# Neighbour maximum in a graph kernel: word numbers added on TensorE, keys by five wide VectorE operations

## What is computed

```
mask = adj != 0
nm[i, f] = max over j with mask[i, j] of x[j, f]      # 0 if the row has no neighbour
x = layernorm(x + nm)
```

## Time and profile before

| | |
|---|---|
| median of 3 runs | 4908.32 us (4907.93 to 4910.63) |
| span of the profiled execution | 5439.8 us |
| PE busy in that span | 4559.6 us (84%) |
| DVE busy | 4311.2 us (79%) |
| ACT busy | 2207.6 us (41%) |
| POOL busy | 1205.9 us (22%) |
| mean granted TensorE clock | 0.929 |

### The profile page before, as it was taken

How to read it: one execution, slowest core, us unless ns; L and a number is a source line. 1 busy time by engine, 2 the same in 40 slices (tenths; PEclk the granted TensorE clock), 3 DMA queues, 4 the chain that set the end, 5 groups by cost and what they waited for, 6 DMA issues and landing times. The chain is left out here.

```text
span 5439.8 us, 68010 instructions
## 1 busy us (share of the span) xinstructions
PE 4559.6 (84%) x22263; PEld 2172.7 (40%) x22263; DVE 4311.2 (79%) x7371; ACT 2207.6 (41%) x2430; POOL 1205.9 (22%) x1342
## 2 busy tenths in 40 slices
PE   4766776677667766579999999999999999999999
PEld 3333333333333333323443333454444445444444
DVE  6666676667666667788888888889999987999998
ACT  3444444444444444398888888410000001000000
POOL 5555445454444455200000000000000000000000
PEclk6888888888888889889999999999999999999999
DMA  7555555555555555233232332122222202212220
GB/s 272 195 187 184 192 197 185 187 182 194 186 179 188 193 169 166 95 130 122 105 126 111 113 127 105 64 102 83 75 84 79 81 9 99 102 70 98 76 96 14
DMA packets 181695, 709.72 MB, mean 130 GB/s; under 512 B 31168, under 2 KB 39872, under 8 KB 132224
## 3 DMA queue, kind: packets, MB, share of 16 engines
q1 hardware_dynamic: 110816, 566.01, 29.3%
q0 software_dynamic: 33760, 73.21, 4.2%
q10 hardware_dynamic: 36864, 67.13, 3.5%
HBM read 630.59 MB, written 79.82 MB: 131 GB/s over the span
## 5 line engine op out<-in xcount | busy, mean ns | idle before, releaser
L1750 PE MATMUL bank<-w,GX 128*128 128x512 f32 x4096 | 1768.4, 593 | 4.8 <-DVE w L1865 4.8
L1865 DVE SCALAR_TENSOR_TENSOR w<-q,E,m 128x512 f32<-128x512 f32 x2048 | 1472.1, 758 | 130.8 <-PE bank L1750 39.1
L356 POOL DMA_INDIRECT ring<-x_ext,idx x1051 | 1032.8, 983 | 1074.2 <-DVE X L619 316.8
L1750 PEld LDWEIGHTS bank<-w,GX 128*128 128x128 f32 x4096 | 777.7, 191 | 975.3 <-issue 975.2
L607 DVE TENSOR_TENSOR top<-top,sums 128x1024 f32<-128x1024 f32 x484 | 589.2, 1217 | 626.7 <-remote 364.8
L507 PE MATMUL sums<-lone,xs 128*128 128x512 fp8e4 x3000 | 838.3, 421 | 287.0 <-DVE top L607 214.9
L1200 PE MATMUL acc<-w,GX 128*128 128x512 f32 x2048 | 939.6, 605 | 65.8 <-DVE w L1458 62.6
L430 ACT ACTIVATE stage<-tp 128x1024 fp8e4<-128x1024 uint16 x512 | 523.7, 1025 | 1088.1 <-remote 598.3
L1458 DVE SCALAR_TENSOR_TENSOR w<-q,E,u 128x1024 f32<-128x1024 f32 x512 | 634.7, 1274 | 1.9 <-PE acc L1200 1.8
L507 PEld LDWEIGHTS sums<-lone,xs 128*128 128x128 bf16 x3000 | 291.5, 105 | 814.7 <-issue 607.4
L1200 PEld LDWEIGHTS acc<-w,GX 128*128 128x128 f32 x2048 | 371.9, 190 | 564.5 <-issue 413.5
(11 more groups left out here) (250 smaller groups left out, 2919.3 us busy)
## 6 DMA issues: line engine op xcount, KB each, us to landing
adjb<-in_adj SPq DMA_DIRECT2D x256, 1024.0 KB
m<-mask_t SPq DMA_DIRECT2D x128, 1024.0 KB, 4.8
mask_t<-stage ACTq DMA_DIRECT2D x256, 256.0 KB
den_m<-mask_t SPq DMA_DIRECT2D x64, 1024.0 KB, 6.9
keep_m<-mask_t SPq DMA_DIRECT2D x64, 1024.0 KB, 4.9
ring<-x_ext,idx POOLq DMA_INDIRECT x1051
z<-row_scores SPq DMA_DIRECT2D x30, 256.0 KB, 4.6
xt_rows<-XT SPq DMA_DIRECT2D x8, 512.0 KB, 4.7
```

What stands on the lines that cost most here:

```text
L356: pool.indirect_dma_start(ring[:, s, :], None, x_ext, bass.IndirectOffsetOnAxis(ap=idx[:, k, s:s + 1], axis=0)).then_inc(done, 16)
L1750: last = nc.tensor.matmul(acc[b][:, :], GX[:, j, :], w[:, j % WR, :], start=(j == 0), stop=(j == T - 1))
L1865: nc.vector.scalar_tensor_tensor(out=w[:, j % WR, :], in0=q, scalar=E[:, j:j + 1], in1=m[:, b, j, :], op0=ALU.max, op1=ALU.mult).then_inc( ...
```

## The change

PE now adds a word's number to its code inside `tally`. Ahead of block 0 and ahead of block 4 of each tile's counts, one matmul with a stationary `one_row` and 512 moving columns of `numbers` starts the bank; the 16-column counts then accumulate onto it. The number is 0 to 255 within each half of the 512 words, times 2^-7. The `opens` activation of ACT is gone. On DVE the wide operations up to the list are now: exponent of the code (TENSOR_SCALAR, in place of L686), code minus it (L706's place), the number OR-ed into 448 of the 512 keys, the minimum of those 448 with `before` (whose nonzero entries are now 2^20), and a MAX8 for each half of 256. L711, L712, L716, L717 and the single MAX8 of L719 go. The release `cnt_used` moves from L706's place to the minimum, since that one still reads `tally`. The sums L701 and L772 go: `due` and `found` come from `accum_out` of the operations before them. The small operations work on 16 values instead of 8 (two on the numbers, the same five in the loop over depth), and their keys (64 with a row of blanks) go into the 64 free places of the 512 keys, so that the sorting rounds run over 512 instead of 536.

```
+LEAST = 2.0
+HALVES = 2
+HW = NW // HALVES
+NUMBER = 2.0 ** -7
+BEFORE = 2.0 ** 20
+MORE = 8 * HALVES
...
@@ POOL, once @@
+            word_steps = Steps(pool, words_numbered)
+            word_steps.did(nc.gpsimd.iota(half_no[:, :, :], pattern=[[HW, HALVES], [0, 8]], base=0, channel_multiplier=0))
+            word_steps.do(nc.gpsimd.memset(one_row_f, 0.0))
+            word_steps.do(nc.gpsimd.affine_select(out=one_row_f, in_=one_row_f, compare_op=ALU.not_equal, fill=1.0, base=0, pattern=[[0, P]], channel_multiplier=1))
...
@@ ACT, phase @@
-                if 1 <= t <= T:
-                    act.wait_ge(counted, t)
-                    nc.scalar.activation(opens[:, :, 1:WPG], before, ACT.Relu, bias=top_bit[:, 0:1], scale=-TOP_BIT).then_inc(opens_made, 1)
...
@@ PE @@
+            pe.wait_ge(numbers_made, 1)
...
             def count(q, k, e):
+                if e % (T // TRB // HALVES) == 0:
+                    bank = slice(e * TRB, e * TRB + T // HALVES)
+                    nc.tensor.matmul(tally[:, bank, :].rearrange("p t c -> p (t c)"), one_row[:, :], numbers[:, :, :].rearrange("p t c -> p (t c)"),
+                                     start=True, stop=False, skip_group_check=True)
                 for g in range(e * TRB, (e + 1) * TRB):
-                    last = nc.tensor.matmul(tally[:, g, :], stage[:, q, g, k * P:(k + 1) * P], powers[:, :], start=True, stop=True)
+                    last = nc.tensor.matmul(tally[:, g, :], stage[:, q, g, k * P:(k + 1) * P], powers[:, :], start=False, stop=True, skip_group_check=True)
...
@@ DVE, once @@
+            steps.did(nc.vector.memset(many_high[:, :, :], 0.0))
+            steps.do(nc.vector.memset(numbers[:, :, :], 0.0))
+            dve.wait_ge(words_numbered, 3)
+            steps.do(nc.vector.tensor_scalar(numbers[:, :, 0:WPG], code_no[:, 0:HW].rearrange("p (t w) -> p t w", w=WPG), NUMBER, None, ALU.mult))
+            nc.vector.tensor_copy(one_row[:, :], one_row_f).then_inc(numbers_made, 1)
...
@@ DVE, phase @@
+                not_opening = keys[:, :, 1:WPG]
+                listed = keys[:, :, :].rearrange("p g w -> p (g w)")
...
                 if extracts:
                     hold(dve, counted, s + 1)
-                    hold(dve, opens_made, s + 1)
-                    steps.did(nc.vector.tensor_tensor(out=bits(by_group(high)), in0=bits(code_ps), in1=bits(opens[:, :, :]), op=ALU.bitwise_and))
-                    side.did(nc.vector.tensor_scalar(junk, cnt, -1.0, 0.0, ALU.add, ALU.max))
+                    steps.did(nc.vector.tensor_scalar(bits(keys[:, :, :]), bits(code_ps), EXPONENT, None, ALU.bitwise_and))
+                    side.did(nc.vector.tensor_scalar(junk, cnt, 1.0, -float(T), ALU.max, ALU.add, accum_out=due[:, bass.ds(s, 1)]))
                     side.did(nc.vector.tensor_reduce(deg[:, bass.ds(s, 1)], cnt, axis=AXX, op=ALU.add))
...
-                if extracts:
-                    side.settle()
-                    side.did(nc.vector.tensor_reduce(due[:, bass.ds(s, 1)], junk, axis=AXX, op=ALU.add))
                 step(1)
                 if extracts:
                     steps.settle()
                     side.settle()
-                    nc.vector.tensor_tensor(out=by_group(x), in0=code_ps, in1=by_group(high), op=ALU.subtract).then_inc(cnt_used, 1)
+                    steps.did(nc.vector.tensor_tensor(out=by_group(x), in0=code_ps, in1=keys[:, :, :], op=ALU.subtract))
+                    steps.settle()
+                    side.did(nc.vector.tensor_tensor(out=bits(not_opening), in0=bits(not_opening), in1=by_group(code_no[:, :])[:, :, 1:WPG], op=ALU.bitwise_or))
                 if finishes:
                     into(old, 0, 2).then_inc(lower_free, 1)
                 if extracts:
-                    hold(dve, cnt_used, s + 2)
-                    steps.do(nc.vector.tensor_scalar(bits(high), bits(x), EXPONENT, None, ALU.bitwise_and))
-                    steps.did(nc.vector.tensor_tensor(out=x, in0=x, in1=high, op=ALU.subtract))
+                    steps.settle()
+                    side.settle()
+                    nc.vector.tensor_tensor(out=not_opening, in0=not_opening, in1=before, op=ALU.min).then_inc(cnt_used, 1)
                 step(2)
                 if extracts:
-                    steps.settle()
-                    steps.did(nc.vector.tensor_tensor(out=bits(x), in0=bits(x), in1=code_no[:, :], op=ALU.bitwise_or))
-                    side.did(nc.vector.tensor_tensor(out=bits(high), in0=bits(high), in1=code_no[:, :], op=ALU.bitwise_or))
-                    steps.settle()
-                    steps.did(nc.vector.max(out=y, in_=x))
+                    for a in range(HALVES):
+                        steps.did(nc.vector.max(out=y[:, 8 * a:8 * a + 8], in_=x[:, a * HW:(a + 1) * HW]))
...
-                    later = keys[:, NW:NW + (DEEP - 1) * MORE].rearrange("p (d n) -> p d n", n=MORE)
+                    later = keys[:, :, 0].rearrange("p (d n) -> p d n", n=MORE)
...
-                    side.did(nc.vector.scalar_tensor_tensor(out=pad[:, :], in0=srt[:, :], scalar=1.0, in1=row_no[:, 0:1].to_broadcast([P, SRT]), op0=ALU.is_lt, op1=ALU.mult))
+                    side.did(nc.vector.scalar_tensor_tensor(out=pad[:, :], in0=srt[:, :], scalar=LEAST, in1=row_no[:, 0:1].to_broadcast([P, SRT]), op0=ALU.is_lt, op1=ALU.mult, accum_out=found[:, bass.ds(s, 1)]))
...
-                    side.did(nc.vector.tensor_reduce(found[:, bass.ds(s, 1)], pad[:, 0:SLOTS], axis=AXX, op=ALU.add))
```

More of the change, by code:

```diff
@@ L206, in neighbour_max @@
         codes = sb("codes", [P, NW], F32)
-        opens = sb("opens", [P, T, WPG], F32)
-        top_bit = sb("top_bit", [P, 1], F32)
-        keys = sb("keys", [P, NW + (DEEP - 1) * MORE], F32)
+        numbers = sb("numbers", [P, T // HALVES, COLS], BF16)
+        one_row = sb("one_row", [P, P], BF16)
+        half_no = sb("half_no", [P, HALVES, 8], I32)
+        keys = sb("keys", [P, T, WPG], F32)
         many = sb("many", [P, MORE], F32)
+        many_i = sb("many_i", [P, MORE], I32)
         many_no = sb("many_no", [P, MORE], I32)
-        many_high = sb("many_high", [P, DEEP - 1, MORE], F32)
+        many_high = sb("many_high", [P, T // MORE, MORE], F32)
         srt = sb("srt", [P, SRT], F32)
@@ L234, in neighbour_max @@
         need_ps = tp[1][0:1, 0, 0:8].bitcast(F32)
-        high = keys[:, 0:NW]
+        one_row_f = merged[:, 2 * P:3 * P]
         low_half = adjb[:, :, :].bitcast(BF16).rearrange("p h (n two) -> p h n two", two=2)[:, :, :, 0]
@@ L252, in neighbour_max @@
         counted = sem("counted")
-        opens_made = sem("opens_made")
-        opens_free = sem("opens_free")
+        words_numbered = sem("words_numbered")
+        numbers_made = sem("numbers_made")
         cnt_used = sem("cnt_used")
@@ L292, in neighbour_max @@
         lowest = codes[:, 0:T]
-        bn = keys[:, 0:6 * T].rearrange("p (t s) -> p t s", s=6)
+        bn = keys[:, :, :].rearrange("p g w -> p (g w)")[:, 0:6 * T].rearrange("p (t s) -> p t s", s=6)
         @block.sync
@@ L657, in row_statistics, with phase @@
                 rows_done.settle()
-            def phase(t, k, extracts=True, finishes=True, quad=None, tops=True):
+            def phase(t, k, extracts=True, finishes=True, quad=None, turned=True):
                 s = t - 1
@@ L663, in phase @@
                 h = HALF
-                tops = tops and quad is not None and k == 0
+                turned = turned and quad is not None and k == 0
                 def bits(ap):
@@ L722, in phase @@
                     steps.settle()
-                    steps.did(nc.vector.tensor_scalar(many_no[:, :], bits(y), NW - 1, None, ALU.bitwise_and))
+                    steps.did(nc.vector.tensor_scalar(many_i[:, :], y, 1.0 / NUMBER, None, ALU.mult))
                 if finishes:
@@ L728, in phase @@
                     steps.settle()
-                    steps.did(nc.vector.tensor_tensor(out=bits(y), in0=bits(y), in1=many_no[:, :], op=ALU.bitwise_xor))
+                    steps.did(nc.vector.scalar_tensor_tensor(out=many_no[:, :], in0=many_i[:, :], scalar=HW - 1, in1=half_no[:, :, :].rearrange("p a n -> p (a n)"),
+                                                             op0=ALU.bitwise_and, op1=ALU.bitwise_or))
                 if finishes:
@@ L750, in phase @@
                 if extracts:
-                    later = keys[:, NW:NW + (DEEP - 1) * MORE].rearrange("p (d n) -> p d n", n=MORE)
-                    steps.did(nc.vector.tensor_tensor(out=bits(later), in0=bits(many_high[:, :, :]), in1=many_no[:, :].unsqueeze(1).to_broadcast([P, DEEP - 1, MORE]), op=ALU.bitwise_or))
+                    later = keys[:, :, 0].rearrange("p (d n) -> p d n", n=MORE)
+                    steps.did(nc.vector.tensor_tensor(out=bits(later), in0=bits(many_high[:, :, :]), in1=many_no[:, :].unsqueeze(1).to_broadcast([P, T // MORE, MORE]), op=ALU.bitwise_or))
+                    hold(dve, cnt_used, s + 2)
                     side.settle()
                     steps.settle()
```

(10 more changed lines are left out.)

14 lines of the change are left out of this document (4 added, 10 removed).

## The result

The changed kernel takes 4935.4 us (median of 4 runs, 4933.1 to 4937.0), the kernel before beside it 4908.1 us: ratio 1.0059, 95% interval 1.0045 to 1.0073. The change makes the kernel slower by about 27 us, and 4937 was forecast.

A forecast was written before the change was run, and what follows sets the result against it. Layer 0 was taken as bound by PE and DVE handing one buffer to and fro. Terms 0.39 + 0.04 + 0.05 = 0.48 us a tile, x 60 = 29 us on 4908.3, gave 4937 us; range 4892 to 4972.

The forecast's parts named there:

- The bound: Layer 0: PE's sums and DVE's maximum hand one buffer to and fro; step floor about 2.85 us, undisturbed tile 24.3 us.
- M(1) to M(3): Between DVE's pair maxima 1 and 3: tally released later, PE's counts wait; +0.39 us a tile, ends -0.08 and 0.70.
- M(7) to M(0): From pair maximum 7 to the next 0, DVE sets the pace: +0.04 us a tile, ends -0.10 and +0.32.
- M(4) to M(5): Between pair maxima 4 and 5, DVE sets the pace: larger small operations, shorter sort, +0.05 us a tile.
- Start: Kernel start: some 1.5 us of added constants and operations, hidden by PE's later wait for adj; 0, ends 0 and 1.5.
- PE's second wide matmul: In step 5, where PE's sums wait 0.89 us for DVE: hidden; without that cover 0.24 us.
- ACT: ACT's L423: ACT has waits to spare, so nothing.
- A: VectorE paces and its shorter list wins: about -15 us, 4893; -80 us, 4828 if DVE's whole sum paces. Chance 0.2.
- B: Delay before the counts is covered by PE's slack, the rest cancels: within 0.2%, near 4910. Chance 0.19.
- E: Remote waits also occur in timed runs and cover the new wait: same as B; no separate chance.
- C: PE idles longer each tile, granted clock falls more often, sums take twice 1.45: +87 us, 4995. Chance 0.04.
- D: `due` and `found` disagree through the accumulators and the fallback runs: milliseconds. Chance under 0.01.

The follow-up runs named there:

- second profile: The kernel before, unchanged, profiled again: 4899.1 us (one run).
- run with ACT's copy: Changed kernel, with ACT copying `before` out of tally at the head of a phase so tally is released after code minus exponent: 4917.8 us, ratio 1.0026.
- run with all moves: Changed kernel, code minus exponent ahead of M(1), count sums behind M(0), numbers and depth steps moved to steps where VectorE idles: 4874.6 us, ratio 0.9944.
- found_off: Run with all moves, plus count sums behind taking over top, `need` as TENSOR_TENSOR, blank slots summed by separate reduction behind M(0); no time of its own given.
- before_both: Kernel before, with tally's release moved to the end of L712 and two wide matmuls a tile adding zeros: 4921.5 us, ratio 1.0038.
- after_no_wide: Changed kernel without PE's wide matmuls, so further-neighbour indices are not right: 4923.3 us, ratio 1.0043.

## Why the prediction was right, and where its terms were off

**The bound.** Right. One buffer passes between PE's sums and DVE's maximum, and a step is the larger of 2.85 us and DVE's list. The tile put together without the remote waits is the tile of the second profile to 0.01 us in every step, as far as it went: it did not resolve the first phases of the quads, nor the phases in which 7 to 0 is longer.

**M(1) to M(3): the wait for tally.** Forecast +0.39 us; measured 3.13 + 3.14 against 3.09 + 2.94, +0.24. The place and the mechanism were right: PE waits 0.94 us, DVE's 1.2 us saved behind M(2) become idle time. Two terms were off, against each other. The counts take 0.40 us, not 0.60: the 0.60 began with weights that were loaded while PE was still busy with the sums, so part of it lay beside them. The wide matmul puts the counts back by 0.22 to 0.23 us (in the changed kernel the first weights are loaded at 1006.57, the first count starts at 1006.80), not 0.10. From the first weights of the counts to the transposes it is 0.61 us instead of 0.70, and PE comes to those weights 0.06 earlier than forecast, counted from M(1): together the 0.15. And what I called one cost, the wait, is a joint one: the wait takes PE's slack and the wide matmul has then none. By the prediction's sum the later release alone costs 0.39 - 0.10 = 0.29 us; alone it cost nothing. The end of the range at -0.08 is reached for M(2) to M(3) in the run with ACT's copy (2.85), though by an earlier release and not by a later arrival of PE.

**M(7) to M(0).** Forecast +0.04; measured +0.11 in first phases; over the others the mean went from 3.79 to 3.89. The exponent operation and the size of the accumulator read were right. That an accumulated sum is an instruction more is what the Trainium skill says (VectorE: DVE Perf Modes, on two Vector instructions with no wait between them), and the trace agrees: DVE_READ_ACCUMULATOR, 83 ns, behind L702 and L780. But the reads cost about 0.01 us each, where I had allowed 0.07, and L772, counted as -0.10, had stood in a wait and cost nothing: without it `idx` starts 0.07 later behind `base`. Two terms of opposite sign were both wrong here.

**M(4) to M(5).** Forecast +0.05; measured +0.13. L764 on 64 elements takes 268 ns, L752 on 24 took 177, and from its start to that of the MAX8 it is 0.40 us instead of 0.28. That is 0.12; the small operations on 16 values add 0.04 in front of it, and the shorter MAX8 takes 0.03 off. I had allowed 0.05 for all of it.

**Start, PE's second wide matmul, ACT.** No cost shows, as forecast. The first maximum is at 101 us against 102, and 5 to 6 and 6 to 7 have not moved. In step 5 the second wide matmul is covered.

**The sum.** Forecast 0.48 us a tile, measured by the first-phase medians 0.24 + 0.11 + 0.13 = 0.48, and 0.02 in M(3) to M(4). By the stretch from M(0) of tile 4 to that of tile 60 it is (1437.5 - 1406.4) / 56 = 0.56. The agreement of the total owes something to luck, since the largest term was 0.15 too high and two small ones together 0.15 too low.

**The rivals.** A (VectorE's shorter list wins) fell: DVE was busy for 64 us less in layer 0 and the time went the other way. The forecast of "some 100 us" less for DVE was too high already by A's own list, 1.3 us x 64 = 83; measured 64. B and E (within 0.2%) fell: the interval begins at 1.0045, and the second profile has no remote waits. C (the clock) fell as it was put: behind the 0.94 us in which PE waits for the minimum the sums take 1.46 us, not twice that, and the granted clock of the stretch is 0.99 in both kernels. But the clock does fall elsewhere, in both kernels (last section). D did not occur.

## What to carry to other kernels

Where two engines hand one buffer to and fro, work taken from an engine counts only in the steps in which its list outlasts the other's turn; look for the idle time between the two and move operations there before making them cheaper (the moves gave 1.2% on top of a change that had lost 0.6%). An early release is worth as much as the slack that it protects: a later release alone cost nothing, an added matmul alone 0.1%, and the two together 0.4%. And a small operation that stands inside a wait can be the cheapest one in the list.

## What was not expected

**A TENSOR_SCALAR waits for POOL's MEMSET, a TENSOR_TENSOR does not.** `need`, on 128x3 numbers in SBUF, took 447 ns in the mean as a TENSOR_SCALAR and up to the end of POOL's MEMSETs (1.02 us at 846.12); as a TENSOR_TENSOR 158 ns. From 200 to 1650 us of the run with all moves it met a MEMSET in 20 of 58 tiles and ended 0.02 to 0.04 us behind the MEMSETs in each, in the other 38 it took 0.17 us; with the other form it met one in 19 of 57 and took 0.16 us in each. The change of form brought 20 us (4867.6 to 4847.4). The kernel before has the same waits (299 ns in the mean, 21 of 58 tiles); the change of form was not tried there. The Trainium skill (SBUF — State Buffer, on who interferes with whom) names `tensor_scalar` among the operations that can take the ports shared with GpSimd for the whole instruction, and says that a TENSOR_TENSOR with two inputs in SBUF contends only with a GpSimd operation that reads. The trace agrees with both: a MEMSET only writes. Which of the two came first it does not settle: the MEMSETs are recorded 0.09 us behind the start of `need`, and records of POOL are rough.

**A profiled execution can be 11% longer than the runs.** Its extra time stood in waits that ended at remote, and in a clock of 0.87 instead of 0.99. The undisturbed tiles in the same trace agreed with the second profile to 0.01 us a step. Why it stalled is open.

**The clock falls at the head of some quads, in every kernel.** In a quad's first phase PE stands still for 2.65 us until DVE has taken over top (L630). Two such places in the second profile of the kernel before, tiles 36 and 40, with the windows of the sums behind them (the clock is the third number from the end):

```profile
910.10 0.62 PE L474 MATMUL tp<-ident_b,adjb 128*128 128x128 bf16 x8 [2.65 <-DVE X L630]
...
910.99 1.46 PE L507 MATMUL sums<-lone,xs 128*128 128x512 fp8e4 x6
...
1009.59 0.62 PE L474 MATMUL tp<-ident_b,adjb 128*128 128x128 bf16 x8 [2.65 <-DVE X L630]
...
1010.48 2.72 PE L507 MATMUL sums<-lone,xs 128*128 128x512 fp8e4 x6
```

```profile
910.90:912.50 1.60, 1.60 (x12) 0.80 (x10) 0.08 (x2) 1.60 (x2) 1.26 (x2) 1.00 0.80 133
1010.40:1013.20 2.80, 2.80 (x10) 1.07 (x8) 0.06 (x1) 1.79 (x2) 2.17 (x3) 0.52 0.74 158
```

In the second the granted clock falls to the lower of its two levels (1.2 GHz) and the sums take 2.72 us instead of 1.46, so that M(0) to M(1) takes 5.51 instead of 4.25. Of the 14 heads of quads from tile 8 to tile 60 this happens at 5 in the kernel before and at 5 in the changed one, and at 4 (found_off) to 12 (before_both, after_no_wide) in the single profiled executions of the other runs. Where the step is short, the granted clock behind PE's wait is 1.00; where it is long, 0.50 to 0.67. A long one costs 0.9 to 2.1 us, so some ten us between two executions can be the clock's and not the change's. What decides it at a given head is open. This is why the steps, which repeat to 0.01 us, settle here what the times alone do not.
